# Cross-attention with a key-axis softmax: two batches take their scale from their own contexts, the others from a later bound over all

## The reference

```python
q = einsum('bte,ef->btf', emb, Wq) + bq          # emb is x: 16 batches, 512 rows, 512 wide
k = einsum('bml,le->bme', latent, Wk) + bk       # latent is ctx: 16 batches, 120 rows, 256 wide
v = einsum('bml,le->bme', latent, Wv) + bv
w = softmax(einsum('bte,bme->btm', q, k) / sqrt(512), axis=1)   # over the 512 rows t, for each m
x = einsum('btm,bme->bte', w, v) + emb
out = (x - mean(x)) * rsqrt(var(x) + 1e-6) * gamma + beta       # over the last axis
```

## Time and profile before

| | |
|---|---|
| median of 3 runs | 218.12 us (217.78 to 218.6) |
| the profiled execution | 218.16 us, its span 216.4 us |
| TensorE matmul busy | 191.5 us, 89% |
| VectorE busy | 178.7 us, 83% |
| ScalarE busy | 162.7 us, 75% |
| GpSimd busy | 146.5 us, 68% |
| moved from and to HBM | 41.04 MB, 190 GB/s |

### The profile page before, as it was taken

How to read it: one execution, slowest core, us unless ns; L and a number is a source line. 1 busy time by engine, 2 the same in 40 slices (tenths; PEclk the granted TensorE clock), 3 DMA queues, 4 the chain that set the end, 5 groups by cost and what they waited for, 6 DMA issues and landing times.

```text
span 216.4 us, 4146 instructions
## 1 busy us (share of the span) xinstructions
PE 191.5 (89%) x1168; PEld 118.5 (55%) x1168; DVE 178.7 (83%) x452; ACT 162.7 (75%) x341; POOL 146.5 (68%) x148
## 2 busy tenths in 40 slices
PE   5699998999999999999999999999999999998000
PEld 4556775474747474647474747474747474634000
DVE  0469767988979898889898988898989899879993
ACT  2455757779797979797979797989797979688510
POOL 1000000039797979798888988797979898978792
PEclk9999999999999999999999999999999999999855
DMA  6999961005475645464555464546564543130454
GB/s 135 327 414 359 383 242 50 3 2 194 168 242 189 226 188 209 174 211 183 211 206 194 194 217 194 204 171 211 211 200 186 191 197 126 50 144 35 182 215 151
DMA packets 10252, 41.04 MB, mean 190 GB/s; under 512 B 1024, under 2 KB 3968, under 8 KB 6272
## 3 DMA queue, kind: packets, MB, share of 16 engines
q1 hardware_dynamic: 9952, 40.37, 50.9%
q10 hardware_dynamic: 288, 0.52, 1.4%
HBM read 24.12 MB, written 16.78 MB: 189 GB/s over the span
## 4 chain that ended last, share of the span: by engine, by line
POOL 47%; issue 14%; PE 13%; DVE 9%; ACT 6%; DMA 6%; DVEq 2%; POOLq 1%; SPq 0%; ACTq 0%
POOL obuf L951 19%; POOL obuf L945 17%; POOL rstd L978 6%; DMA wq_nat<-in_L_xattn_Wq 4%; ACT obuf L612 3%; PE s_ps L427 3%; POOL square_mean L964 3%; PE g_ps L365 2%; DVE obuf L819 2%; DMA out<-obuf 2%; PE s_ps L365 2%; ACT xT L551 1%; DVEq L78 1%; PE xT_ps L359 1%; PE g_ps L397 1%
## 5 line engine op out<-in xcount | busy, mean ns | idle before, releaser
L945 POOL TENSOR_TENSOR obuf<-obuf,gamma_all 128x512 f32<-128x512 f32 x44 | 59.4, 1375 | 17.5 <-ACT obuf L612 17.5
L427 PE MATMUL s_ps<-xT,gT 128*120 128x512 f32 x128 | 57.8, 593 | 0.1
L951 POOL TENSOR_TENSOR obuf<-obuf,beta_all 128x1536 f32<-128x1536 f32 (+1 forms) x16 | 51.7, 3231 | 1.2
L551 ACT ACTIVATE xT<-xT_ps 128x512 f32<-128x512 f32 x64 | 34.4, 588 | 4.4 <-PE xT_ps L405 4.2
L427 PEld LDWEIGHTS s_ps<-xT,gT 128*120 128x120 f32 x128 | 23.2, 183 | 26.2 <-issue 17.9
L419 PE MATMUL pv_ps<-v_part,prob_part 120*128 120x512 f16 x135 | 35.7, 381 | 2.0 <-ACT prob_part L599 0.7
L612 ACT ACTIVATE obuf<-xbuf,shift,rstd 128x512 f32<-128x512 f32 x44 | 32.7, 805 | 5.5 <-POOL shift L983 5.2
L405 PEld LDWEIGHTS xT_ps<-ident,xbuf 128*128 128x128 f32 x256 | 29.8, 140 | 9.9 <-issue 7.5
L405 PE MATMUL xT_ps<-ident,xbuf 128*128 128x128 f32 x256 | 33.2, 273 | 0.0
L830 DVE SCALAR_TENSOR_TENSOR xbuf<-pv_ps,back_y,xbuf 128x512 f32<-128x512 f32 x45 | 32.5, 746 | 0.0
L603 ACT ACTIVATE square_junk<-xbuf,neg_mean 128x512 f32<-128x512 f32 x36 | 25.7, 717 | 3.6 <-DVE neg_mean L838 3.2
(11 more groups left out here) (124 smaller groups left out, 266.3 us busy)
## 6 DMA issues: line engine op xcount, KB each, us to landing
xbuf<-in_x SPq DMA_DIRECT2D x16, 1024.0 KB, 4.8
out<-obuf SPq DMA_DIRECT2D x14, 1024.0 KB, 4.2
out<-obuf SPq DMA_DIRECT2D x8, 256.0 KB, 2.5
ctx_nat<-in_ctx SPq DMA_DIRECT2D x16, 120.0 KB, 4.2
wq_nat<-in_L_xattn_Wq SPq DMA_DIRECT2D x2, 512.0 KB, 9.1
obuf<-in_ctx SPq DMA_DIRECT2D x1, 1024.0 KB, 10.3
obuf<-in_ctx SPq DMA_DIRECT2D x1, 896.0 KB, 12.0
wk_nat<-in_L_xattn_Wk SPq DMA_DIRECT2D x1, 512.0 KB, 6.1
```

Of the source, the lines that this page charges most:

```text
L427: mm = pe.matmul(s_ps[0:M, :], gT[:, k % 2, e, :], xT[:, e, :], start=(e == 0), stop=(e == EC - 1))
L551: act.activation(xT[:, e, :].rearrange("p (j q) -> p j q", q=P), xT_ps[e % 2][:], ACT.Copy)\
L945: pool.tensor_tensor(obuf[:, k % 2, j, :], obuf[:, k % 2, j, :], gamma_all[:], ALU.mult)\
L951: done = pool.tensor_tensor(obuf[:, k % 2, 0:share, :], obuf[:, k % 2, 0:share, :], beta_all[:].unsqueeze(1).broadcast_to([P, share, E]), ...
```

## The change

The contexts of batches 0 and 1 get a scale of their own (`scale[:, 0]`), from the largest absolute value in just these two, as they lie in `ctx_nat`. All others take `scale[:, 4]`, from the sums over all contexts, which now belong to the second all-reduce. `back_g`, `back_v` and `onto_v` get a second column for it. Around this, the loads, the fillers and the instructions of the prologue and of ScalarE's slot 1 change their order, and `keep_warm` changes its counts. The diff below goes through the names, then SP's queue, TensorE, ScalarE, VectorE and GpSimd in this order; left out are the sizes of the small tiles.

```diff
-WK, WQ, WV = CTX_PARTS, CTX_PARTS + 1, CTX_PARTS + 2
+FIRST_CTX, WK, WQ, ALL_CTX, WV = 0, 1, 2, 3, 3 + CTX_PARTS
+OWN_SCALE = 2
...
+        def of_ctx_scale(b):
+
+            return 0 if isinstance(b, int) and b < OWN_SCALE else 1
+
+        def ctx_scale(b):
+            return scale[:, 0:1] if of_ctx_scale(b) == 0 else scale[:, 4:5]
...
             load_ctx(0, 0)
+            load_ctx(1, 1)
+            sp.dma_start(wv[:], Wv.rearrange("(c p) e -> p c e", p=P)).then_inc(wv_in, 16)
+            load_x(0, 0)
+            sp.dma_start(bv_all[:], bv.partition_broadcast(P)).then_inc(bv_in, 16)
             flat = ctx_in.rearrange("b m l -> (b m l)").rearrange("(p q) -> p q", p=P)
             for h in range(2):
                 q = slice(CTX_EDGES[h * CTX_PARTS // 2], CTX_EDGES[(h + 1) * CTX_PARTS // 2])
                 sp.dma_start(ctx_all[:, q], flat[:, q]).then_inc(ctx_all_in[h], 16)
-            load_x(0, 0)
-            sp.dma_start(wv[:], Wv.rearrange("(c p) e -> p c e", p=P)).then_inc(wv_in, 16)
-            load_ctx(1, 1)
-            sp.dma_start(bv_all[:], bv.partition_broadcast(P)).then_inc(bv_in, 16)
...
-            keep_warm(12, g_ps)
+            keep_warm(25, g_ps)
             pe.wait_ge(wk_in, 16)
...
-            keep_warm(3, g_ps)
+            keep_warm(9, g_ps)
             pe.wait_ge(wq_in[0], 16)
...
             def context_g(b, k):
                 pe.wait_ge(ctx_low, b + 1)
+                if is_slot(b, 0):
+                    pe.wait_ge(high_split, 2)
+                    pe.wait_ge(low_split, 2)
                 if is_in(b, 1, B):
...
-            pe.wait_ge(ones_set, 1)
-            pe.wait_ge(w_diag_done, LC)
-            for c in range(LC):
-                mm = pe.matmul(w_row[:, c * P:(c + 1) * P], ones[:], w_diag[:, c, :], start=True, stop=True)
-            mm.then_inc(w_spread, 1)
             multiply_qk(2)
             multiply_qk(3)
 
-            keep_warm(9, pv_ps[0])
             pe.wait_ge(wT_copied, 2 + FC)
             pe.wait_ge(x_in[0], 16)
             turn_x(0, 0, 0)
             turn_x(0, 0, 1)
-            pe.wait_ge(high_split, 2)
-            pe.wait_ge(low_split, 2)
             context_g(0, 0)
             turn_x(0, 0, 2)
             turn_x(0, 0, 3)
+            pe.wait_ge(ones_set, 1)
+            pe.wait_ge(w_diag_done, LC)
+            pe.wait_ge(ctx_low, 1)
+            for c in range(LC):
+                mm = pe.matmul(w_row[:, c * P:(c + 1) * P], ones[:], w_diag[:, c, :], start=True, stop=True)
+            mm.then_inc(w_spread, 1)
             turn_ctx(1, 1, 0)
             scores(0, 0)
             context_g(1, 1)
...
             copy_wqT(2)
-            sum_ctx(0)
             copy_wqT(3)
-            sum_ctx(1)
...
             def copy_g(b, k):
                 act.wait_ge(g_done, b + 1)
+                if is_slot(b, OWN_SCALE):
+                    act.wait_ge(back_done, 2)
                 for e in range(EC):
-                    act.activation(gT[:, k % 2, e, :], g_v[:, e, :], ACT.Identity, scale=back_g[:],
+                    act.activation(gT[:, k % 2, e, :], g_v[:, e, :], ACT.Identity,
+                                   scale=back_g[:, of_ctx_scale(b):of_ctx_scale(b) + 1],
                                    bias=u_col[:, e:e + 1]).then_inc(g_copied, 1)
...
             copy_xT(0, 0)
             copy_xT(0, 1)
+            sum_ctx(0)
             act.wait_ge(back_done, 1)
             act.wait_ge(dots_done, LC + 1 + EC)
...
-                if main:
+                if main and not is_slot(s, 1):
                     copy_xT(s, 0)
                     copy_xT(s, 1)
...
                     if is_slot(s, 1):
                         v_to_high(0, 0)
                         ctx_to_high(2, 2)
+                        copy_xT(1, 0)
                     probs_to_high(s - 1)
+                    if is_slot(s, 1):
+                        copy_xT(1, 1)
                 if main:
...
             largest(own_bound[:, WQ:WQ + 1], wq_nat[:].rearrange("p c e -> p (c e)"))
+            for b in range(OWN_SCALE):
+                dve.wait_ge(ctx_loaded[b], 16)
+            dve.tensor_reduce(own_bound[0:M, FIRST_CTX:FIRST_CTX + 1], ctx_nat[:, 0:OWN_SCALE, 0:L], AX.XY, ALU.max,
+                              apply_absolute_value=True).then_inc(dve_bounds, 1)
             for c in range(EC // 2):
                 dot(LC + c, wq_nat[:, c], bk_all, u_col[:, c:c + 1])
-            dve.wait_ge(ctx_all_in[1], 16)
-            for h in range(2, CTX_PARTS):
-                dve.tensor_reduce(own_bound[:, h:h + 1], ctx_all[:, CTX_EDGES[h]:CTX_EDGES[h + 1]],
-                                  AX.X, ALU.add, apply_absolute_value=True).then_inc(dve_bounds, 1)
-            for c in range(EC // 2, EC):
-                dot(LC + c, wq_nat[:, c], bk_all, u_col[:, c:c + 1])
-            dve.wait_ge(w_spread, 1)
-            dve.tensor_copy(w_row[:, L:L + 1], d_col[0:M, :]).then_inc(w_row_done, 1)
...
             dve.wait_ge(max_bounds, 1)
-            dve.tensor_reduce(bound[:, 0:1], max_bound[:, 0:CTX_PARTS], AX.X, ALU.max)
+            dve.tensor_copy(bound[:, 0:1], max_bound[:, FIRST_CTX:FIRST_CTX + 1])
             scales(dve.tensor_tensor(bound[:, 1:2], max_bound[:, WQ:WQ + 1], max_bound[:, WK:WK + 1], ALU.mult))
             exact_scales(0, 2)
-            dve.scalar_tensor_tensor(back_g[:], back[:, 0:1], -SCALE, back[:, 1:2], ALU.mult, ALU.mult)\
+            dve.scalar_tensor_tensor(back_g[:, 0:1], back[:, 0:1], -SCALE, back[:, 1:2], ALU.mult, ALU.mult)\
                 .then_inc(back_done, 1)
             dve.wait_ge(scales_done, 1)
...
+            for c in range(EC // 2, EC):
+                dot(LC + c, wq_nat[:, c], bk_all, u_col[:, c:c + 1])
             ctx_to_low(0, 0)
+            dve.wait_ge(wv_in, 16)
+            largest(own_bound[:, WV:WV + 1], wv[:].rearrange("p c e -> p (c e)"))
             low_part(qk_part[:, LOW, 0, :], g_ps[:], scale[:, 1:2], qk_part[:, HIGH, 0, :], 1)
             low_part(qk_part[:, LOW, 1, :], s_ps[:], scale[:, 1:2], qk_part[:, HIGH, 1, :], 2)
-            dve.wait_ge(wv_in, 16)
-            largest(own_bound[:, WV:WV + 1], wv[:].rearrange("p c e -> p (c e)"))
             dve.wait_ge(bv_in, 16)
             largest(bv_bound[:], bv_all[:])
+            for h in range(1, CTX_PARTS):
+                dve.wait_ge(ctx_all_in[h * 2 // CTX_PARTS], 16)
+                dve.tensor_reduce(own_bound[:, ALL_CTX + h:ALL_CTX + h + 1], ctx_all[:, CTX_EDGES[h]:CTX_EDGES[h + 1]],
+                                  AX.X, ALU.add, apply_absolute_value=True).then_inc(dve_bounds, 1)
 
             dve.wait_ge(max_bounds, 2)
+            scales(dve.tensor_reduce(bound[:, 4:5], max_bound[:, ALL_CTX:ALL_CTX + CTX_PARTS], AX.X, ALU.max))
             dve.tensor_copy(bound[:, 2:3], max_bound[:, WV:WV + 1])
-            dve.wait_ge(dve_bounds, 5)
-            scales(dve.scalar_tensor_tensor(bound[:, 3:4], bound[:, 0:1], max_bound[:, WV:WV + 1], bv_bound[:],
+            dve.wait_ge(dve_bounds, 4)
+            scales(dve.scalar_tensor_tensor(bound[:, 3:4], bound[:, 4:5], max_bound[:, WV:WV + 1], bv_bound[:],
                                             ALU.mult, ALU.add))
-            exact_scales(2, 4)
+            exact_scales(2, 5)
             dve.wait_ge(scales_done, 2)
+            ctx_to_low(1, 1)
+            dve.scalar_tensor_tensor(back_g[:, 1:2], back[:, 4:5], -SCALE, back[:, 1:2], ALU.mult, ALU.mult)\
+                .then_inc(back_done, 1)
             dve.tensor_scalar(back_y[:], back[:, 3:4], 1.0 / PROB_SCALE, None, ALU.mult)
+            dve.tensor_tensor(back_v[:, 0:1], back[:, 0:1], back[:, 2:3], ALU.mult)
+            scales(dve.tensor_tensor(back_v[:, 1:2], back[:, 4:5], back[:, 2:3], ALU.mult))
+            dve.tensor_scalar(onto_v[:], back_v[:], scale[:, 3:4], None, ALU.mult)
             dve.tensor_scalar(bv_scaled[:], bv_all[:], scale[:, 3:4], None, ALU.mult)
-            scales(dve.tensor_tensor(back_v[:], back[:, 0:1], back[:, 2:3], ALU.mult))
-            ctx_to_low(1, 1)
-            dve.tensor_tensor(onto_v[:], back_v[:], scale[:, 3:4], ALU.mult)
+            dve.wait_ge(w_spread, 1)
+            dve.tensor_copy(w_row[:, L:L + 1], d_col[0:M, :]).then_inc(w_row_done, 1)
 
             def key_bias(b, k, r):
...
             def scale_v(b):
                 dve.wait_ge(v_done, b + 1)
-                dve.scalar_tensor_tensor(v_bank(b)[0:M, :], v_bank(b)[0:M, :], onto_v[0:M, :], bv_scaled[0:M, :],
+                dve.scalar_tensor_tensor(v_bank(b)[0:M, :], v_bank(b)[0:M, :],
+                                         onto_v[0:M, of_ctx_scale(b):of_ctx_scale(b) + 1], bv_scaled[0:M, :],
                                          ALU.mult, ALU.add).then_inc(v_copied, 1)
...
-            pool.wait_ge(act_bounds, 3)
-            pool.wait_ge(dve_bounds, 3)
-            pool.partition_all_reduce(max_bound[:, 0:WV], own_bound[:, 0:WV], P, bass.bass_isa.ReduceOp.max)\
-                .then_inc(max_bounds, 1)
```

(38 more changed lines are left out.)

## The result

The changed kernel takes 216.75 us (median of 6 runs, 216.47 to 217.17), the kernel before 217.81 (217.72 to 218.6, with the three runs known earlier). The ratio, which goes by means, is 0.9945, with a 95% interval of 0.9929 to 0.9962: 1.1 us faster by the medians and 1.2 by the ratio, clear of no change. The forecast was 217.7, no change that can be told. The profiled execution took 216.94, its span 215.1, against 218.16 and 216.4.

The account below looks back on a forecast made before the run. GpSimd's loop ring was taken as the bound, and the change could only move its first turn. From 218.16, 0.1 lost at v(0) and 0.46 gained in slot 1 gave 217.8, taken as 217.7 with v(0) unmoved; range 216.7 to 218.7.

Parts of the forecast that it names:

- The early part: Prologue up to g(0): first two contexts' scale no longer waits for all sums, more fillers; g(0) 1.8 us early.
- g(0): TensorE's product of batch 0's context with the combined weight; foreseen near 21.1 instead of 22.88, set by VectorE's second low part.
- The DMA order: ctx(1), Wv, x(0), bv load ahead of all contexts, whose last load lands at 21.5, needed about 22.5; no cost.
- rival 2: Slower: fillers stay at the slow pace and delay Wk's and Wq's transposes; full price 1.25 us, 219.4; chance 0.08.
- Slot 1: ScalarE runs exponential(0) ahead of batch 1's two xT copies; probabilities-times-v product and scores(1) 0.46 us earlier, reaching the ring.
- the ring: Loop cycle of GpSimd's gamma, beta and rstd work through ScalarE's normalise; untouched by the diff, only its first turn can move.
- rival 4: Slot 1's gain is swallowed by slot 2, GpSimd's first gamma stays at 48.25; 218.2; chance 0.08.
- v(0): TensorE's product of batch 0's context with Wv; waits for low_part(wv) in VectorE's queue; foreseen unmoved at 30.0 to 30.1.
- The sum: VectorE's queue ahead of low_part(wv): 2.80 us added against 2.70 of idle removed, so low_part(wv) starts at 28.4.
- g(1): TensorE's product of batch 1's context with the combined weight; foreseen at 28.4, TensorE then standing 1.6 us.
- rival 1: TensorE, not VectorE's queue, sets v(0), at most 1.6 us early; 216.1 to 217.0, around 216.7; chance 0.24.
- Rival 3: The second all-reduce, which VectorE waits for, takes its upper bound, 0.41 us more; 218.1, no change; chance 0.10.

Follow-up runs that it names:

- key_bias behind: The changed kernel with w_row's last column and key_bias(0) moved behind low_part(wv) on VectorE; median 216.25 us, ratio 0.9918 to the kernel before.
- kernel before, new loads: The kernel before with only ctx(1), Wv, x(0) and bv loaded ahead of the two loads of all contexts; median 224.65 us, ratio 1.0278.

## Why the prediction was wrong

The forecast was no change that can be told, and the change is clear: 216.75 lies in the stated range by 0.05 only.

**The early part: right in its times, not in what held g(0).** g(0) was foreseen near 21.1 and came at 20.55, which is 20.84 with the 0.29 of Wq's landing put back. The first product, foreseen at 11.0, came at 10.66, with Wq's first half 0.47 earlier. The DMA order cost nothing. "ScalarE has the high part ready at 19.9, so VectorE sets it" did not hold: the high part ended at 19.61 and VectorE's low part started at 19.66, both queues ready within 0.05. In all nine profiles with the split bound the low part starts 0.03 to 0.05 behind the end of the high part, and g(0) starts 9.88 or 9.89 behind the first pass of the product. So TensorE's products were on the path after all: level with VectorE to 0.04 in five of the nine, the first profile among them, and later in the other four.

That the clock would be up before Wq held in all profiles with 25 fillers (rival 2 fell), and the profiles of the changed kernel had its rise at 5.5, 7.5 and 7.9. (The Trainium skill, "TensorE: Matmul & The Clock Gate", section "What's actually happening", says that the point of the rise varies from run to run. By that rule, the traces agree; the half microsecond that the page gives for it does not hold here, where it is 2.4 us between three profiles of one kernel.) But the spread worked the other way. It sits in the kernel before, which at times loses another 1.1 us, and the fillers take it away. The forecast had only weighed what fillers can cost.

**Slot 1: right.** 0.51 for 0.46, in both kernels, and it reached the ring unchanged, 8.41 to 8.43 from scores(1) to the first gamma in every profile (rival 4 fell).

**v(0): the step that failed.** "The sum is 2.80 against 2.70: low_part(wv) starts at 28.4, v(0) at 30.0 to 30.1 as before." Counted from VectorE's first instruction on Wq, this put low_part(wv) 0.10 later; it came 0.29 earlier (0.1 to 0.3 over three profiles). And v(0) came 0.54 earlier (0.34 to 0.54). The sum was 0.4 too high, and it set v(0) by VectorE alone, before and after. Two terms were off, and a third was put at nothing.

- The idle that goes was 3.2, not 2.70. I added the three idle stretches of VectorE's rows. A row's idle runs from the end of the one before, but an instruction that waits for nothing starts some 0.08 before that end (one of 0.17 at 25.60, the next at 25.68 in the changed kernel): 0.24 for three. And two waits too short to be listed: ctx_to_low(0) to the first low part took 0.50 and now takes 0.38, key_bias(0) to low_part(wv) 0.52 and now 0.35. The latter was a wait for ScalarE's high part of Wv, which ended at 28.25. The work added was 2.9, close to the 2.80. Of the 0.39, 0.30 shows already at the second low part of the combined weight (19.66, where 20.25 less the 0.29 was foreseen).
- Before, v(0) did not start when low_part(wv) was done. That ended at 29.57, and v(0) started at 29.92, directly behind g(1), whose 24 passes take 1.26 from their start to the next: 1.63 from the one start to the other, in every profile with the old order on time. In the changed kernel it is 1.38. TensorE was the later of the two by 0.25, so with TensorE early, v(0) gains 0.25 without VectorE being any faster. I had set both kernels' v(0) by VectorE, and read g(1) only in the sum for the new one.
- The fillers were counted for the product and put at nothing for v(0), since VectorE's queue was to set it. But the 0.29 is what VectorE gains when TensorE's products don't hold it. The wait for ScalarE's high parts, which stand behind these products, adds 0.14 and 0.20 to low_part(wv) in the other two profiles of the changed kernel, and 0.47 and 0.52 in the two with the old fillers. From g(0) on, v(0) follows at 8.54 or 8.55 in all of them. With the old fillers nothing of the 0.54 is left (18.36 against 18.38).

Together 0.29 + 0.25 = 0.54, and 0.49 from slot 1 in this pair, are 1.03 in the trace, against a fall of the medians by 1.06. The forecast had 0.46 of it. The ratio says 1.2; that the rest is long runs of the kernel before, as the one of 218.6 in that series, is not shown. This is rival 1 in kind, TensorE's lead reaching v(0), but in a middle form that I hadn't written down: before, TensorE is last by 0.25, and now VectorE is last, with TensorE standing 0.90 (over a microsecond was foreseen). A third of the lead's 1.6 gets through. That VectorE's queue is what v(0) waits for from g(0) on is shown by the run with key_bias behind.

**Rival 3** (the bare all-reduce at its upper end) fell: 0.57 from the last sum's end to VectorE's next instruction, 0.5 foreseen.

## What to carry to other kernels

Where two engines meet at a wait, write down for both the time at which they would be ready, before and after; the one that is late by 0.3 us is a term of its own. Count idle time on an in-order engine from start to start against a stretch of the same instructions that runs without waits, not from the listed gaps. Fillers that keep TensorE's clock up are worth what the runs cost in which the clock comes late or is lost again, and one profile of a good run doesn't show that; the granted clock of the single runs does. And when an edit brings nothing alone, try it with the one that it makes room for: here the split bound and the fillers, neither moving v(0) alone, moved it by 0.5 together.

## What was not expected of the hardware

- A wait of 2 us on TensorE was followed by a stretch at half clock, twice in one profile (kernel before, new loads), and the second cost 1.6 us on top of the wait. By their times four of the six runs bear that cost and two don't.
- The same program (the kernel before) had its first rise of the clock between 4.6 and 6.5 us in one profile and at 12.6 in the other, and in the first case lost it again at 8.3. Twelve of its 64 runs have the mean granted clock of that long profile.
- The second half of Wq landed anywhere from 10.95 to 11.58 over fourteen profiles in which the same loads stood ahead of it.
